# Score products on the two halves of the array's rows, with both maxima taken side by side, in a cross-attention and mixture-of-experts kernel

## The reference

```python
q = (layernorm(x) @ q_w.T + q_b).reshape(B, S, H, d).transpose(0, 2, 1, 3)
k = (ctx[:, :100] @ k_w.T + k_b) ...            # the window never reaches past token 99
v = (ctx[:, :100] @ v_w.T + v_b) ...
q = apply_rope(q) * d ** (-0.5)
k = apply_rope(k)
scores = where(0 <= q_pos - k_pos <= 64, q @ k.T, -inf)      # per head, 100 x 100
e = exp(scores - max(scores))
ctx = (e / e.sum()) @ v
x = x + ctx @ o_w.T + o_b
x = x + experts(layernorm(x))                   # router, top 2 of 8, silu(gate) * up, down
```

## Time and profile before

| what | value |
|---|---|
| three timed runs | 503.87, 501.49, 498.05 us; median 501.49 us |
| the profiled execution | 498.88 us |
| its span, first to last instruction | 496.9 us |
| PE busy | 444.2 us (89%) |
| DVE busy | 301.7 us (61%) |
| ACT busy | 270.8 us (54%) |
| POOL busy | 118.4 us (24%) |
| granted TensorE clock, mean | 0.961 |

### The profile page before, as it was taken

One profiled execution on the slowest core, in us unless ns is written; L12 is line 12 of the kernel. 1 busy time (PEld: TensorE's weight loads), 2 busy tenths in 40 slices (PEclk: granted clock), 3 DMA queues, 4 the chain that ended last, 5 costly groups with the idle time before them and its releaser, 6 DMA issues.

```text
span 496.9 us, 8810 instructions
## 1 busy us (share of the span) xinstructions
PE 444.2 (89%) x2747; PEld 365.4 (74%) x2747; DVE 301.7 (61%) x727; ACT 270.8 (54%) x853; POOL 118.4 (24%) x118
## 2 busy tenths in 40 slices
PE   3897999999999998309999999999999999999980
PEld 2655675656666654208999999999999999999980
DVE  3664869797887966873746646557376473663330
ACT  1286877787778687404545546455454463643330
POOL 5201014141514214530004041050320402204013
PEclk9999999999999999657999999999999999999995
DMA  7074301020202111157655546554566453213003
GB/s 237 25 209 142 135 22 52 21 64 8 62 12 57 27 41 52 41 153 265 234 160 123 163 105 164 180 98 154 133 149 201 80 168 93 30 39 38 1 1 36
DMA packets 24317, 49.36 MB, mean 99 GB/s; under 512 B 5368, under 2 KB 15160, under 8 KB 24140
## 3 DMA queue, kind: packets, MB, share of 16 engines
q10 hardware_dynamic: 7886, 26.44, 17.2%
q1 hardware_dynamic: 10238, 15.36, 10.3%
q0 software_dynamic: 6144, 6.97, 8.6%
HBM read 38.51 MB, written 12.74 MB: 103 GB/s over the span
## 4 chain that ended last, share of the span: by engine, by line
PE 73%; DVE 7%; ACT 6%; issue 4%; POOL 3%; DMA 3%; SPq 2%; ACTq 1%; POOLq 0%; DVEq 0%
PE b_o L634 9%; PE b_small L634 9%; PE b_s L621 8%; PE b_s L622 8%; PE b_s L623 8%; PE b_s L420 6%; ACT probs L749 4%; PE b_pv L443 3%; PE b_pt L621 3%; PE b_pt L623 3%; PE b_pt L622 3%; PE b_pt L429 3%; PE b_proj L474 3%; PE b_proj L498 2%; PE b_s L418 2%
## 5 line engine op out<-in xcount | busy, mean ns | idle before, releaser
L749 ACT ACTIVATE probs<-b_s,negmax 100x100 f32<-100x100 f32 x256 | 85.6, 361 | 24.1 <-DVE negmax L1003 21.2
L1191 POOL DMA_INDIRECT out<-y_sb,idnow x32 | 48.7, 1522 | 180.5 <-ACT y_sb L790 173.1
L778 ACT CAST h_hi<-h_sb 128x448 fp32r<-128x448 f32 x64 | 36.3, 567 | 86.5 <-DVE h_sb L1094 86.5
L621 PE MATMUL b_s<-x_hi,w_hi 128*128 128x448 f32 x192 | 72.2, 376 | 0.7 <-DVE x_lo L1084 0.7
L622 PE MATMUL b_s<-x_lo,w_hi 128*128 128x448 f32 x192 | 71.3, 371 | 0.0
L623 PE MATMUL b_s<-x_hi,w_lo 128*128 128x448 f32 x192 | 71.1, 370 | 0.0
L981 DVE TENSOR_TENSOR w_lo<-w_raw,w_hi 128x1024 fp32r<-128x1024 f32 x48 | 58.4, 1224 | 13.6 <-ACT w_hi L713 13.6
L1098 DVE TENSOR_TENSOR h_lo<-h_sb,h_hi 128x448 fp32r<-128x448 f32 x64 | 40.2, 628 | 40.5 <-ACT h_hi L778 40.5
L749 ACT ACTIVATION_READ_ACCUMULATOR probs<-b_s,negmax 100x1 f32 x256 | 57.1, 223 | 0.0
L420 PE MATMUL b_s<-kblk,qrot 128*100 128x400 f32 x128 | 53.7, 500 | 0.0
L1003 DVE TENSOR_REDUCE negmax<-b_s 100x4 f32<-100x400 f32 x64 | 36.2, 566 | 27.0 <-PE b_s L420 26.3
(11 more groups left out here) (131 smaller groups left out, 930.2 us busy)
## 6 DMA issues: line engine op xcount, KB each, us to landing
w_raw<-in_ffw ACTq DMA_DIRECT2D x48, 512.0 KB, 3.9
xin<-slots SPq DMA_DIRECT2D x9, 449.8 KB, 4.6
slots<-in_padrows SPq DMA_DIRECT2D x8, 449.8 KB, 4.6
kblk<-krot SPq DMA_DIRECT2D x128, 12.5 KB, 1.8
out<-x_all SPq DMA_DIRECT2D x8, 200.0 KB
ctx_all<-in_ctxT SPq DMA_DIRECT2D x1, 1200.0 KB, 6.3
x_all<-in_x SPq DMA_DIRECT2D x1, 1200.0 KB
attw<-in_wT ACTq DMA_DIRECT2D x2, 256.0 KB, 3.7
```

Of the source, the lines that this page charges most:

```text
L621: pe.matmul(o, wh[:, c, cols], x_hi[:, c, :], start=(c == 0), stop=False)
L749: m = nc.scalar.activation(probs[:, N % 3, h, :], b_s[N % 3][0:S, h * S:(h + 1) * S], ACT.Exp, bias=negmax[:, N % 4, h:h + 1], accum_out=p ...
L778: nc.scalar.copy(h_hi[:, f, :], h_sb[:, f % 2, :]).then_inc(s_hhi, 1)
L1191: G.indirect_dma_start(out, bass.IndirectOffsetOnAxis(idnow[:, n:n + 1], 0), y_sb[:, n, :], None, bounds_check=TOK + TILE - 1, oob_is_err= ...
```

## The change

Keys of heads 4 to 7 of a chunk go into the same four column blocks as heads 0 to 3 (`h % QH`); they occupy rows 64 to 127, the others rows 0 to 63. `kblk` is half as wide. `scores` runs in even slots only and does groups n and n + 1: two mask products into two banks, then two score products, one on rows 0 to 63 and one on rows 64 to 127. Its second mask product waits for the exponentials of group n - 2. DVE takes the two maxima one behind the other, in the even slots. The key projection and its evacuation move from slot 1 to slot 0, the key rotation from slot 2 to slot 1, and `places` from slot 5, ahead of the query rotation, to slot 6, behind the maxima.

```diff
@@ -186,7 +186,7 @@
-        kblk = att_sb("kblk", [P, 2, DC, HC, PT])
+        kblk = att_sb("kblk", [P, 2, DC, QH, PT])
@@ -341,7 +341,7 @@
                     for h in range(HC):
                         r = slice(h * DH, (h + 1) * DH)
-                        sp.dma_start(kblk[r, i % 2, c, h, :],
+                        sp.dma_start(kblk[r, i % 2, c, h % QH, :],
@@ -404,22 +404,25 @@
             def scores(i, n):
-                N = NQ * i + n
                 b, s = quad(n)
                 c = s * QH // HC
-                h = s * QH % HC
                 if n == 0:
                     pe.wait_ge(s_qrot, i + 1)
                 if n in (0, HC // QH):
                     pe.wait_ge(s_kblk[c], 16 * HC * (i + 1))
-                if N >= 3:
-                    pe.wait_ge(s_p, N - 2)
-                o = b_s[N % 3][0:S, 0:QH * S]
-                pe.matmul(o, ident_bf[0:S, 0:S], mask_bf[0:S].rearrange("p h s -> p (h s)"),
-                          start=True, stop=False)
-                pe.matmul(o, qrot[:, i % 2, 2 * c + b, :],
-                          kblk[:, i % 2, c, h:h + QH, b * S:(b + 1) * S],
-                          start=False, stop=True).then_inc(s_s, 1)
+                banks = []
+                for m in range(2):
+                    N = NQ * i + n + m
+                    if N >= 3:
+                        pe.wait_ge(s_p, N - 2)
+                    banks.append(b_s[N % 3][0:S, 0:QH * S])
+                    pe.matmul(banks[m], ident_bf[0:S, 0:S], mask_bf[0:S].rearrange("p h s -> p (h s)"),
+                              start=True, stop=False)
+                for m in range(2):
+                    r = slice(m * P // 2, (m + 1) * P // 2)
+                    pe.matmul(banks[m], qrot[r, i % 2, 2 * c + b, :],
+                              kblk[r, i % 2, c, :, b * S:(b + 1) * S],
+                              start=False, stop=True).then_inc(s_s, 1)
@@ -562,7 +565,7 @@
-                    if cur:
+                    if cur and n % 2 == 0:
                         scores(i, n)
@@ -580,7 +583,7 @@
-                    if n == (0 if i < 0 else 1) and nxt:
+                    if n == 0 and nxt:
                         k_project(i + 1)
@@ -996,12 +999,12 @@
-                    if cur:
-                        v.wait_ge(s_s, N + 1)
-                        if N >= 4:
-                            v.wait_ge(s_p, N - 3)
-                        V.tensor_reduce(negmax[:, N % 4, :],
-                                        b_s[N % 3][0:S, 0:QH * S].rearrange("p (h s) -> p h s", h=QH),
+                    for M in (N, N + 1) if cur and n % 2 == 0 else ():
+                        v.wait_ge(s_s, M + 1)
+                        if M >= 4:
+                            v.wait_ge(s_p, M - 3)
+                        V.tensor_reduce(negmax[:, M % 4, :],
+                                        b_s[M % 3][0:S, 0:QH * S].rearrange("p (h s) -> p h s", h=QH),
                                         AX.X, ALU.max, negate=True).then_inc(s_max, 1)
@@ -1009,7 +1012,7 @@
-                    if n == (0 if i < 0 else 2) and nxt:
+                    if n == (0 if i < 0 else 1) and nxt:
                         k_rotate(i + 1)
@@ -1022,10 +1025,10 @@
-                    if n == 5 and 0 <= i - 2 < NPAIR:
-                        places(i - 2)
                     if n == 5 and nxt:
                         q_rotate(i + 1)
+                    if n == 6 and 0 <= i - 2 < NPAIR:
+                        places(i - 2)
```

## The result

The changed kernel takes 516.24 us (median of 4 runs, 515.97 to 517.34) against 501.64 us for the kernel before in the same session: a ratio of 1.030, 95% interval 1.024 to 1.037. The forecast was 504.0, within 496.5 to 515, so it is slower by 3% and outside the range. The profiled execution took 515.97 us with a span of 514.1 us.

The account below looks back on a forecast made before the run. PE was taken to lead in attention, DVE close behind. Pairs 2 to 6 +3.0, pair 1 -0.7, pair 7 +1.3: +3.6 on the profiled 498.88 makes 502.5, raised to 504 as that execution was fast; range 496.5 to 515.

Parts of the forecast that it names:

- first stretch: Attention, values product of group 4 to scores of group 4: two pairs of groups, 12.66 us instead of 13.38.
- nothing new is late: Same stretch: score pairs wait for exponentials of two groups back, as the transposes already did, so no added delay.
- -0.7: Pair 1, which has no places step: a period of 21.7 us, 0.7 us less.
- Scores side by side: Score products on PE: both row halves run together in 0.67 us, a pair of groups 1.39 us against 1.76.
- A: Rival, score products: row halves do not run together, 0.67 us more a pair, some +12 us, 516; chance 0.08.
- B: Rival, score products: strict program order makes a pair take three pass times, 0.33 us more, +7, 511; chance 0.05.
- The second stretch: Attention, scores of group 4 to next values product: PE's denominator transpose waits for places, 10.27 us instead of 9.03.
- The stall of 0.1 us at POOL's rows: PE's transposes wait for normalised rows behind POOL's scatters and inverse deviation: 0.1 us, 0 to 0.5 by spread.
- The sum: Attention: a full period 23.0 us instead of 22.4, +3.0 over pairs 2 to 6; in all +3.6.
- +1.3: Pair 7, the end: nothing is rotated, but the last attend stands behind one more maximum and places, +1.3 us.
- main case: Whole kernel: the change makes it slower by 3.6 us, forecast 504, own range 500 to 508; chance 0.51.

Follow-up runs that it names:

- The bank read alone: Changed kernel with only the first instruction of places, the read of the small bank, back in slot 5 ahead of the query rotation: 507.83 us, ratio 1.014.

## Why the prediction was wrong

The span grew by 17.2 us where 3.6 were forecast. Two steps of the prediction failed. It said of the first stretch "nothing new is late", and late signals took 4.6 us there. And it gave pair 1 "-0.7" without a term for ACT's six issues or for the clock, which together took up to 7.4 us in pairs 1, 2 and 7. A third term was too small: the first stretch was to save 0.74 us and saved 0.36, 1.9 us over five periods.

**Scores side by side: right.** 1.39 us a pair was forecast and 1.32 measured; "row halves do not run together" (A, 2.1) and the strict order (B, 1.7) are out. B was my reading of the program-order rule in the Trainium skill (TensorE: Matmul & The Clock Gate, Part 3, What overlaps and what doesn't). The records do not name a pass's product, so the rule may stand; the price I drew from it, a third pass time, does not.

**The second stretch: right in mechanism and size.** 10.27 forecast, 10.39 measured, with the wait on `places` where it was put. The bank read alone shows its price, 0.70 us of a period.

**The first stretch, "nothing new is late": the step that failed from pair 4 on.** The stall of 0.1 us at POOL's rows is not what was wrong. The rows met PE as walked: xn's transposes start 5.69 us after the values product (143.98 - 138.29), as 6.06 - 0.37 had it. But moving `places` moved the scatters to the front of slot 0, and the signals of that slot came up to 1.5 us late. The prediction priced the scatters only as work ahead of rstd in POOL's queue. The late signals cost 1.03 to 1.07 us in each of pairs 4 to 6 and 1.5 in pair 7. A smaller part of that stretch was also too low: two pairs were to save 2 x 0.37 = 0.74 of 12.92 from mask to mask, and 12.56 is what the kernel with `places` in slot 5 needs. The row halves gave 0.70 there, as said, but the new order took 0.34 back; of its parts only the forward move of the keys was tried alone, and it cost 0.74 in the old order. With 1.03 for the signals this makes the 1.4 us by which the stretch is longer than walked.

**The sum.** A full period was to be 23.0 and is 24.44. Pair 3, which has the bank wait and almost no late signals, takes 23.41, so without them the forecast would have been 0.4 too low. The kernel without the bank wait comes to 22.99, but that this is the forecast number is luck, since the forecast has the wait in it. With `places` in slot 5 it is 22.85.

**Pair 1, "-0.7": wrong sign.** From first mask to first mask it took 26.19 us against 22.79, 3.4 more. PE stands still for 2.82 us behind ACT's weight issues (1.97 before) and then runs at a granted clock of 0.50, the 1.2 GHz level, until 55.6 us, where the kernel before keeps 1.00. The prediction had no term for the issues and none for the clock. Without the issues the pair takes 20.65 us in the changed kernel and 20.63 in the kernel before, so a forecast of no change would have been right for it. Windows of the changed kernel show the half clock twice more:

```profile
86.30:89.70 3.40, 3.25 (x9) 2.43 (x10) 2.52 (x11) 2.03 (x10) 2.03 (x2) 0.51 0.20 60
209.20:212.60 3.40, 3.40 (x16) 2.31 (x15) 1.06 (x5) 2.77 (x13) 2.74 (x3) 0.50 0.31 85
```

At half the clock 3.4 us do the work of 1.7, so these two cost up to 1.7 us each. The first did cost 1.6: the second stretch of pair 2 takes 12.47 us, the others 10.86. Why the clock fell in these two places is not shown.

**The end, "+1.3": measured +4.5.** It holds another 1.5 us of late signals (pair 7's slot 0) and up to 1.7 us of the half clock at 209.20.

Where 17.2 us of span went, by the differences from first mask to first mask of each pair: 3.6 as forecast; pair 1, 4.1 more than forecast; pair 2, 2.0 (most of it clock); pair 3, 0.3; pairs 4 to 6, 1.4 each; the end 3.2. That makes 17.4. The chance of 0.32 for slower by over 1% named A, B and the upper third of the main case; what came was none of these mechanisms.

**What stays open.** That late signals follow the scatters is shown by moving these: they went when the step went back, came with it into the old order, and moved along when POOL's order changed. In the table the last of them is raised 4.9 to 6.3 us after the first scatter's start in every kernel that has any. That the distance alone does not decide is shown too. The kernel before has none, with signals due 5.1 and 5.5 us after its first scatter; with the weight loads by SP and the same distances it has some. So what makes a signal late is not known, and no run changed the transfers themselves.

## What to carry to other kernels

A step that is moved takes along everything that it lets go: here one small DVE step held a PSUM bank that PE wanted and four DMAs of POOL, and a saving of 0.8 us a period from the row halves was lost twice over (0.57 and 1.02 us). Ask of a moved step who reads the bank and what starts behind it, and split it if these want different places. Look at what an engine issues as well as at what it computes: moving six DMA issues out of ACT's queue was worth more (0.7%) than anything that the change gave in time. And compare the granted clock in two traces before their waits: a half clock of a few us turned up in another pair, or in none, with each new order.

## What the runs showed of the hardware

- PE's signals came 0.1 to 1.9 us after the modelled end of a product while the next products started on time. In the rows this looks like a wait for PE with no work in it (2.28 us before the copy at 142.48).
- Two products on rows 0 to 63 and 64 to 127 run together: 0.92 us for both, each of two passes with 400 columns.
- The Trainium skill (DMA: Bandwidth & Descriptors, Issuing engines are not separate DMA queues) says that spreading DMAs over engines saves only the time to initiate them, "which is usually small relative to the DMA itself". That is the saving seen here, and on the path it was not small: 3.17 us for six issues, and a ratio of 0.993.
- A copy of `rdenx` on DVE takes 0.29 us, but 1.30 in the changed kernel at 143.84, beside POOL's addition (143.72 to 144.99). The Trainium skill (Advanced Engine Details and Errata, VectorE Performance Modes) says that the second SBUF port of the Vector engine is shared with GpSimd, and that GpSimd instructions and those Vector instructions that run in a two-port mode block each other. The rows agree, though none of them names the mode in which the copy ran.
- After a standstill of 2.8 us PE was granted 0.50 until 55.6 us, for some 5.6 us of work. The same half clock turned up elsewhere when the order changed, and in one kernel it lasted 23 us and outweighed a shorter period.
